# Two contraction stages cut into twice as many passes with operands loaded two passes ahead, and a shorter recurrence of powers

## The chip, the cores and the metric

The kernel runs on one Trainium2 chip, on all 8 of its cores at once. Each core has five engines: TensorE (PE: matmuls, with its weight loads PEld), VectorE (DVE), ScalarE (ACT), GpSimd (POOL) and SyncE (SP). The last two only issue DMAs here. The metric is the device time in microseconds of the slowest core, and lower is better. The cores don't exchange anything: each takes 2,048 of the 16,384 tokens.

## The reference

The input is x with 16,384 tokens of width 4,096 (H). Cut to what matters:

```python
xn = layernorm(x)
# attention-like part: S = 1024, F = 9984, G = 6
approx_up = xn @ up_w.T
delta = xn @ gate_w.T - local_point
keep = abs(delta) <= 2.5
out = approx_up @ local_approx_output.T
for m in 1..6:
    tmp = delta**m / m! * approx_up        # written with exp, log and the sign
    if m > 4: tmp = tmp * keep
    out = out + tmp @ fuse_weight[:, :, m - 1].T
s = out + (silu(xn @ ffn_gate_w.T) * (xn @ ffn_up_w.T)) @ ffn_down_w.T
# second part: base weights plus a mixture of low-rank experts
g = silu(xn @ W_base.T + b_base + moe(xn))
result = x + s * g
```

## The kernel before

The whole kernel is the function `build` of before.py. It has no scheduler: `Prog.emit` appends each instruction to the list of its engine in program order, with the semaphores that it waits for and those that it increments, and each engine works its list strictly in order. `dma` (line 154) is the helper behind every transfer, so all transfers have that line. SP's transfers go through a hardware queue. GpSimd's go through a software queue; it takes all loads that cast float32 weights to bfloat16, and the stores that add to what DRAM holds.

A core's data stand feature-major: 128 partitions of features or of contraction, 2,048 tokens along the free axis. `xnbuf` holds 32 blocks of 2,048 tokens in bfloat16. `wbufA` and `wbufB` hold weight tiles in turn, the PSUM tensors `P0` and `P1` (2,048 columns of float32 each) take the results of groups in turn. The stages, in order:

- ln and moe (from line 193): layer norm in place in `xnbuf`, the router and the low-rank part.
- g (line 444): g for 32 blocks of 128 output rows, to `g_d` in DRAM.
- B (line 510): for 8 blocks of S and 2 halves of the tokens (16 half-tiles) the matmuls of `approx_up` (L565) and `gate` (L580), then on VectorE the powers of delta times `approx_up`, each scaled and cast by ScalarE and stored by SP to `tmp_d`, seven operands of 8 blocks.
- D (line 675): for 78 blocks of F the gate and up matmuls (L722, L736), the product to `a_d`.
- C (line 778): the seven operands of `tmp_d` times `w7b`, contraction 7 x 1,024, into `s_d`.
- E (line 867): `a_d` times `wdb`, contraction 9,984, added into `s_d`, and in its last pass the result.

The whole of `tmp_d` or `a_d` doesn't fit into `xnbuf`, so C and E go in passes over the contraction. C has 2 passes (called C0 and C1 here) of 28 contraction blocks, E has 3 (E0 to E2) of 26. At the start of a pass SP loads its operands, filling nearly all of `xnbuf`, in 7 or 5 transfers; they wait for the last matmul of the pass before (`w_ops`). The pass then runs over 32 blocks of 128 output rows (`hc`). A group, which is one `hc` in one pass, has 4 x 28 matmuls (C, line 841) or 4 x 26 (E, line 942) into one PSUM tensor. Its weight tile is issued by `emit_cload` or `emit_eload` when group hc - 2 has ended; the tiles of the first two groups wait for the last group of the pass before:

```python
if hc >= 2:
    w.append(("MM", grp[hc - 2]))
else:
    w.append(("MM", t_mm_d_last if pz == 0 else gpp))
```

Behind each group ScalarE copies PSUM to the one staging tile `stf` (L856, L958), and GpSimd stores `stf` to `s_d[hc]`: plainly in C0, with `accum_op=ALU.add` in C1, E0 and E1. The copy waits for the store before it (`gs_tok[hc - 1]`), as there is one `stf`. On GpSimd's list the weight load for hc + 2 stands ahead of the store of hc.

In the last pass of E nothing is accumulated in DRAM. For each group SP loads `s_d`, `g_d` (into the last quarter of `xnbuf`) and `x_fm` (into `stf`), VectorE adds PSUM to s (L978), multiplies with g (L982), adds x (L985), and SP stores `stf` to `out`. The load of x into `stf` waits for the store of the group before (`os_out[hc - 1]`), the load of s for its last VectorE operation.

## Time and profile before

| what | value |
|---|---|
| three runs | 10157.4, 12016.82, 12089.78 us (median 12016.82) |
| profiled execution, time | 10159.01 us |
| its span on the slowest core | 10157.5 us |
| spans of the eight cores | 10128.5 to 10157.5 us |
| mean granted TensorE clock | 0.969 to 0.971 of full speed |
| busy in the span | PE 9528.4, PEld 4305.5, DVE 782.6, ACT 707.4, POOL 709.6 us |
| HBM | 917.81 MB read, 271.58 MB written per core |

The profiled execution stands with the fastest of the three runs. The span is from the first to the last instruction of a core; the launch adds little to it (1.5 us here). By the timeline D ends at about 6125 us, C0 starts at 6166, C1 at 7018, E0 at 7853, E1 at 8636, E2 at 9425.

How to read it: busy time of an engine matters only where that engine sets the pace. The list of waits says what ended an engine's idle time. In the timeline, pieces of equal instructions are merged, and "SPq" or "POOL ... DMA_DIRECT2D" is the issuing of a transfer, not the transfer itself; its landing is in the list of DMA issues, in us from the issue. KB there count what is written, so a cast weight tile reads twice that.

### The profile page before, as it was taken

To read this page: it belongs to the slowest core of one execution; us is meant where nothing else is said; L and a number is where in the kernel's file an instruction comes from. 1 tells how busy PE (TensorE), PEld (TensorE's weight loads), DVE (VectorE), ACT (ScalarE), POOL (GpSimd) and SP (SyncE) were. 2 spreads that over 40 slices of the span, in tenths; PEclk is the share of its full clock that TensorE was granted. 3 is DMA by queue.
4 is the path that set the end of the run, shared out by engine and by line. 5 is a ranking of instruction groups with operands and counts; after the bars stand their busy time and mean duration, and the time that the engine had idled before them with its cause. 6 is when DMAs were issued, how large, how long until landed. Compare 5 with 4: busy or idle time off the path is not lost.

```text
span 10157.5 us, 93330 instructions; the slowest of 8 cores (10128.5 to 10157.5 us)
## 1 busy us (share of the span) xinstructions
PE 9528.4 (94%) x43089; PEld 4305.5 (42%) x43960; DVE 782.6 (8%) x560; ACT 707.4 (7%) x510; POOL 709.6 (7%) x534
## 2 busy tenths in 40 slices
PE   4799989899999999999999997997997997998899
PEld 1344434344444444444444443443443443443344
DVE  1200035000000000000000000000000000000233
ACT  2000023000000000000000000000000000000000
POOL 0000000000000000000000000000100110010000
PEclk6899999999999999999999998998998998999999
DMA  5155565443443434434344435556566666566888
...
DMA packets 1486876, 822.07 MB, mean 81 GB/s; under 512 B 1403671, under 2 KB 1403928, under 8 KB 1449496
## 3 DMA queue, kind: packets, MB, share of 16 engines
...
q14 instruction: 41, 0.34, 0.0%
HBM read 917.81 MB, written 271.58 MB: 117 GB/s over the span
## 4 chain that ended last, share of the span: by engine, by line
PE 93%; another core or an unknown queue 2%; DMA 2%; DVE 1%; issue 1%; ACT 0%; SPq 0%; POOL 0%; DVEq 0%; ACTq 0%; POOLq 0%
PE P L942 21%; PE P L722 21%; PE P L736 21%; PE P L841 15%; PE P L478 9%; PE P L565 2%; PE P L580 2%; DMA xnbuf<-x_fm 1%; DVE xnbuf L292 0%; DVE xnbuf L298 0%; DMA xnbuf<-tmp_d 0%; ACT scr L213 0%; PE P L230 0%; DMA wbufA<-wub 0%
## 5 line engine op out<-in xcount | busy, mean ns | idle before, releaser
L942 PE MATMUL P<-xnbuf,wbufA 128*128 128x512 bf16 x4893 | 1086.9, 381 | 194.1 <-DMA wbufA<-wdb 188.9
L722 PE MATMUL P<-xnbuf,wbufA 128*128 128x512 bf16 x4893 | 1087.0, 380 | 37.4 <-DMA wbufA<-wub 32.2
L736 PE MATMUL P<-xnbuf,wbufA 128*128 128x512 bf16 x4892 | 1084.4, 379 | 5.3
L736 PE MATMUL P<-xnbuf,wbufB 128*128 128x512 bf16 x4892 | 1084.4, 379 | 5.3
L722 PE MATMUL P<-xnbuf,wbufB 128*128 128x512 bf16 x4892 | 1084.2, 379 | 5.3
L942 PE MATMUL P<-xnbuf,wbufB 128*128 128x512 bf16 x4892 | 1079.7, 379 | 5.3
L841 PE MATMUL P<-xnbuf,wbufA 128*128 128x512 bf16 x3513 | 781.2, 381 | 119.5 <-DMA wbufA<-w7b 103.2
L942 PEld LDWEIGHTS P<-xnbuf,wbufA 128*128 128x128 bf16 x4992 | 489.9, 98 | 783.9 <-issue 199.8
L841 PE MATMUL P<-xnbuf,wbufB 128*128 128x512 bf16 x3511 | 774.6, 379 | 3.8
L722 PEld LDWEIGHTS P<-xnbuf,wbufA 128*128 128x128 bf16 x4992 | 488.5, 98 | 623.8 <-issue 36.0
L736 PEld LDWEIGHTS P<-xnbuf,wbufA 128*128 128x128 bf16 x4992 | 488.9, 98 | 588.6
L736 PEld LDWEIGHTS P<-xnbuf,wbufB 128*128 128x128 bf16 x4992 | 488.9, 98 | 588.6
L942 PEld LDWEIGHTS P<-xnbuf,wbufB 128*128 128x128 bf16 x4992 | 488.5, 98 | 589.0
L722 PEld LDWEIGHTS P<-xnbuf,wbufB 128*128 128x128 bf16 x4992 | 488.0, 98 | 589.4
L841 PEld LDWEIGHTS P<-xnbuf,wbufA 128*128 128x128 bf16 x3584 | 351.6, 98 | 544.3 <-issue 125.8
L841 PEld LDWEIGHTS P<-xnbuf,wbufB 128*128 128x128 bf16 x3584 | 350.7, 98 | 422.9
L764 DVE TENSOR_TENSOR bfst<-scr,P 128x1024 bf16<-128x1024 f32 x156 | 190.5, 1221 | 4136.0 <-PE P L736 4136.0
L478 PE MATMUL P<-xnbuf,wbufA 128*128 128x512 bf16 x2007 | 452.0, 380 | 5.1 <-DVE scr L426 3.0
L478 PE MATMUL P<-xnbuf,wbufB 128*128 128x512 bf16 x2006 | 449.9, 379 | 2.2
L753 ACT ACTIVATE scr<-P 128x1024 f32<-128x1024 f32 x156 | 159.7, 1024 | 4151.4 <-PE P L722 4151.4
L978 DVE TENSOR_TENSOR xnbuf<-P,xnbuf 128x2048 f32<-128x2048 f32 x32 | 73.3, 2292 | 3800.0 <-PE P L942 3625.3
L478 PEld LDWEIGHTS P<-xnbuf,wbufA 128*128 128x128 bf16 x2048 | 200.9, 98 | 246.3 <-issue 6.3
...
## 6 DMA issues: line engine op xcount, KB each, us to landing
s_d<-stf POOLq DMA_DIRECT2D x128, 1024.0 KB, 13.1
wbufA<-wgb POOLq DMA_DIRECT2D x39, 1024.0 KB, 14.0
wbufA<-wub POOLq DMA_DIRECT2D x39, 1024.0 KB, 18.1
wbufB<-wgb POOLq DMA_DIRECT2D x39, 1024.0 KB, 14.0
wbufB<-wub POOLq DMA_DIRECT2D x39, 1024.0 KB, 18.0
...
```

What stands on the lines that cost most here:

```text
L478: lambda e, buf=buf, P=P, kc=kc, c0=c0: e.matmul(P[:, c0:c0 + 512], buf[:, kc * 128:(kc + 1) * 128], xn(kc, c0, 512), start=(kc == 0), sto ...
L565: e.matmul(P[:, pc:pc + 512], buf[:, kc * 128:(kc + 1) * 128], xn(kc, c0, 512), start=(kc == 0), stop=(kc == KC - 1)),
L580: e.matmul(P[:, pc:pc + 512], buf[:, 4096 + kc * 128: 4096 + (kc + 1) * 128], xn(kc, c0, 512), start=(kc == 0), stop=(kc == KC - 1)),
L722: pc=ntl * 512: e.matmul(P[:, pc:pc + 512], buf[:, kc * 128:(kc + 1) * 128], xn(kc, c0, 512), start=(kc == 0), stop=(kc == KC - 1)),
L736: pc=1024 + ntl * 512: e.matmul(P[:, pc:pc + 512], buf[:, 4096 + kc * 128: 4096 + (kc + 1) * 128], xn(kc, c0, 512), start=(kc == 0), stop= ...
L753: lambda e, P=P, sgs=sgs: e.activation(sgs, P[:, 0:1024], AF.Silu),
L764: e.tensor_tensor(abuf[:, t0:t0 + 1024], sgs, P[:, 1024:2048], ALU.mult),
L841: sp=(op == 6 and scl == 3): e.matmul(P[:, c0:c0 + 512], buf[:, j * 128:(j + 1) * 128], cop(j, c0, 512), start=st, stop=sp),
L942: e.matmul(P[:, c0:c0 + 512], buf[:, fsc * 128:(fsc + 1) * 128], cop(fsc, c0, 512), start=(fsc == 0), stop=(fsc == 25)),
L978: lambda e, P=P: e.tensor_tensor(s_ld, P[:, :], s_ld, ALU.add),
```

## The change

Four things are changed.

- C gets 4 passes of 14 contraction blocks, E 6 of 13. Group sizes are 4 x 14 and 4 x 13 matmuls, weight tiles 448 and 416 KB instead of 896 and 832. `w7b` and `wdb` are laid out on the host to fit.
- `xnbuf` is split into region A and region B. Pass n uses A if it is even, B if it is odd. The operands of the first two passes of a stage are issued at its start, and those of pass n + 2 behind pass n, waiting for its last matmul (`grp_pass[pz - 2]`). Semaphores LA and LB replace OL.
- The stores with accumulation are now those of C1 to C3 and E0 to E4; the final arithmetic is in E5. The weight tiles of a pass's first two groups wait, as before, for the last group of the pass before.
- In B each power comes from the product before it (`ts_b = delta * ts_a` and so on), without the separate chain of powers; the absolute value goes to `dpA`, right behind delta, and the mask is applied once to the fifth product.

```diff
-    w7b = nc.dram_tensor("w7b", [2, KC, 7, 4, 128, 128], F32, **EI)
+    w7b = nc.dram_tensor("w7b", [4, KC, 7, 2, 128, 128], F32, **EI)
...
-    wdb = nc.dram_tensor("wdb", [3, KC, 26, 128, 128], F32, **EI)
+    wdb = nc.dram_tensor("wdb", [6, KC, 13, 128, 128], F32, **EI)
...
+                t = p.emit("scalar", lambda e: e.activation(dpA, delta, AF.Abs),
+                           wait=[("AC", t_ac_delta)])
+                t_ac_abs = t["AC"]
                 tt = p.emit("vector", lambda e: e.tensor_mul(ts_a, delta, au_f),
                             wait=[("AC", t_ac_delta), ("EV", t_ev_auf)],
                             inc=[("EV", 1)])
                 t_ac1 = store_op(1, ts_a, tt["EV"])
-                p.emit("vector", lambda e: e.tensor_mul(dpA, delta, delta))
-                tt = p.emit("vector", lambda e: e.tensor_mul(ts_b, dpA, au_f),
+                tt = p.emit("vector", lambda e: e.tensor_mul(ts_b, delta, ts_a),
                             inc=[("EV", 1)])
                 t_ac2 = store_op(2, ts_b, tt["EV"])
-                p.emit("vector", lambda e: e.tensor_mul(dpB, dpA, delta))
-                tt = p.emit("vector", lambda e: e.tensor_mul(ts_a, dpB, au_f),
+                p.emit("vector",
+                       lambda e: e.tensor_single_scalar(dpA, dpA, 2.5,
+                                                        ALU.is_le),
+                       wait=[("AC", t_ac_abs)])
+                tt = p.emit("vector", lambda e: e.tensor_mul(ts_a, delta, ts_b),
                             wait=[("AC", t_ac1)], inc=[("EV", 1)])
                 t_ac3 = store_op(3, ts_a, tt["EV"])
-                p.emit("vector", lambda e: e.tensor_mul(dpA, dpB, delta))
-                tt = p.emit("vector", lambda e: e.tensor_mul(ts_b, dpA, au_f),
+                tt = p.emit("vector", lambda e: e.tensor_mul(ts_b, delta, ts_a),
                             wait=[("AC", t_ac2)], inc=[("EV", 1)])
                 t_ac4 = store_op(4, ts_b, tt["EV"])
-                p.emit("vector", lambda e: e.tensor_mul(dpB, dpA, delta))
-                t = p.emit("scalar", lambda e: e.activation(ts_b, delta, AF.Abs),
-                           wait=[("AC", t_ac4)])
-                t_ac_abs = t["AC"]
-                p.emit("vector",
-                       lambda e: e.tensor_single_scalar(ts_b, ts_b, 2.5,
-                                                        ALU.is_le),
-                       wait=[("AC", t_ac_abs)])
-                p.emit("vector", lambda e: e.tensor_mul(dpB, dpB, ts_b))
-                tt = p.emit("vector", lambda e: e.tensor_mul(ts_a, dpB, au_f),
+                p.emit("vector", lambda e: e.tensor_mul(dpB, delta, ts_b))
+                tt = p.emit("vector", lambda e: e.tensor_mul(ts_a, dpB, dpA),
                             wait=[("AC", t_ac3)], inc=[("EV", 1)])
                 t_ac5 = store_op(5, ts_a, tt["EV"])
-                p.emit("vector", lambda e: e.tensor_mul(dpA, dpB, delta))
-                tt = p.emit("vector", lambda e: e.tensor_mul(ts_b, dpA, au_f),
+                tt = p.emit("vector", lambda e: e.tensor_mul(ts_b, delta, ts_a),
                             wait=[("AC", t_ac4)], inc=[("EV", 1)])
                 t_ac6 = store_op(6, ts_b, tt["EV"])
...
+        def emit_c_oploads(pz):
+            reg = "AB"[pz % 2]
+            w = [("MM", grp_pass[pz - 2]), ("DBG", t_dbg_ln)]
+            w += [("TS%d" % i, t_ts_final[i]) for i in range(4)]
+            base = (pz % 2) * 28672
             for op in range(7):
-                sem_o = "OL%d" % op
+                sem_o = "L%s%d" % (reg, op)
                 tt = dma("sync", sem_o,
-                         xnbuf[:, op * 8192:(op + 1) * 8192].rearrange(
-                             "p (s t) -> p s t", s=4),
-                         tmp_d[op, pz * 4:(pz + 1) * 4].rearrange(
+                         xnbuf[:, base + op * 4096: base + (op + 1) * 4096]
+                         .rearrange("p (s t) -> p s t", s=2),
+                         tmp_d[op, pz * 2:(pz + 1) * 2].rearrange(
                              "s p t -> p s t"),
-                         wait=w_ops)
-                ol_tok[op] = tt[sem_o]
-
+                         wait=w)
+                ol_tok[(pz, op)] = (sem_o, tt[sem_o])
+
+        def emit_cwload(pz, hc, grp, wtok):
+            w = []
+            if hc >= 2:
+                w.append(("MM", grp[hc - 2]))
+            else:
+                w.append(("MM", grp_pass[pz - 1]))
+            buf = [wbufA, wbufB][hc % 2]
+            sem = ["WA", "WB"][hc % 2]
+            tt = dma("gpsimd", sem,
+                     buf[:, 0:1792].rearrange("p (j m) -> p j m", j=14),
+                     w7b[pz, hc].rearrange("o s p m -> p (o s) m"), wait=w)
+            wtok[hc] = tt[sem]
+
+        emit_c_oploads(0)
+        emit_c_oploads(1)
+        for pz in range(4):
+            base = (pz % 2) * 28672
...
+            emit_cwload(pz, 0, grp, wtok)
+            emit_cwload(pz, 1, grp, wtok)
...
+            if pz + 2 < 4:
+                emit_c_oploads(pz + 2)
...
+        grp_pass = {-2: c_regA_last, -1: c_regB_last}
...
+        def emit_e_oploads(tz):
+            reg = "AB"[tz % 2]
+            w = [("MM", grp_pass[tz - 2]), ("AS0", t_as_final[0]),
+                 ("AS1", t_as_final[1])]
...
+        for tz in range(6):
...
-                if tz < 2:
+                if tz < 5:
...
+            if tz + 2 < 6:
+                emit_e_oploads(tz + 2)
```

`emit_ewload` and the rest of `emit_e_oploads` are built like their twins in C.

Three places of the order of instructions, before and now. First SP, from the first operand load of C to the first load of the final arithmetic; `xnbuf<-tmp_d` are operands of C, `xnbuf<-a_d` of E. Before:

```order
L154 DMA xnbuf<-tmp_d 128x4x2048 [waits MM,TS0,TS1,TS2,TS3]
L154 DMA xnbuf<-tmp_d 128x4x2048 x6
L154 DMA xnbuf<-tmp_d 128x4x2048 [waits MM]
L154 DMA xnbuf<-tmp_d 128x4x2048 x6
L154 DMA xnbuf<-a_d 128x6x2048 [waits MM,AS0,AS1]
L154 DMA xnbuf<-a_d 128x5x2048 x4
L154 DMA xnbuf<-a_d 128x6x2048 [waits MM]
L154 DMA xnbuf<-a_d 128x5x2048 x4
L154 DMA xnbuf<-a_d 128x6x2048 [waits MM]
L154 DMA xnbuf<-a_d 128x5x2048 x4
L154 DMA xnbuf<-s_d 128x2048 [waits GS]
```

Now:

```order
L155 DMA xnbuf<-tmp_d 128x2x2048 [waits MM,TS0,TS1,TS2,TS3]
L155 DMA xnbuf<-tmp_d 128x2x2048 x13
L155 DMA xnbuf<-tmp_d 128x2x2048 [waits MM]
L155 DMA xnbuf<-tmp_d 128x2x2048 x6
L155 DMA xnbuf<-tmp_d 128x2x2048 [waits MM]
L155 DMA xnbuf<-tmp_d 128x2x2048 x6
L155 DMA xnbuf<-a_d 128x5x2048 [waits MM,AS0,AS1]
L155 DMA xnbuf<-a_d 128x4x2048 x2
L155 DMA xnbuf<-a_d 128x5x2048 [waits MM]
L155 DMA xnbuf<-a_d 128x4x2048 x2
```

Each load had waited for the end of the pass just before its own. Now the first wait covers two passes of C, and each later set stands behind the end of the pass two before its own. Four more pairs of rows with `xnbuf<-a_d`, for E2 to E5, follow in the second list.

Second GpSimd, from the last groups of C0 to the first groups of C1. Before:

```order
L154 DMA s_d<-stf 128x2048 [waits AC]
L154 DMA wbufB<-w7b 128x28x128 [waits MM]
L154 DMA s_d<-stf 128x2048 [waits AC] x3
L154 DMA wbufA<-w7b 128x28x128 [waits MM]
L154 DMA wbufB<-w7b 128x28x128
L154 DMA wbufA<-w7b 128x28x128 [waits MM]
L154 DMA s_d<-stf 128x2048 [waits AC]
```

Now:

```order
L155 DMA s_d<-stf 128x2048 [waits AC]
L155 DMA wbufB<-w7b 128x14x128 [waits MM]
L155 DMA s_d<-stf 128x2048 [waits AC] x3
L155 DMA wbufA<-w7b 128x14x128 [waits MM]
L155 DMA wbufB<-w7b 128x14x128
L155 DMA wbufA<-w7b 128x14x128 [waits MM]
L155 DMA s_d<-stf 128x2048 [waits AC]
```

Nothing has moved here: two weight tiles stand behind the last three stores. They have half the size, and the first still waits for TensorE's count. This piece now comes nine times in C and E instead of four.

Third VectorE, one half-tile of B, from the copy of `approx_up` (all names in it are parts of `scr`). Before:

```order
L631 TENSOR_TENSOR scr<-scr 128x1024 [waits AC,EV]
L635 TENSOR_TENSOR scr<-scr 128x1024 [waits EV]
L636 TENSOR_TENSOR scr<-scr 128x1024 [waits EV]
L639 TENSOR_TENSOR scr<-scr 128x1024 [waits EV]
L640 TENSOR_TENSOR scr<-scr 128x1024 [waits AC,EV]
L643 TENSOR_TENSOR scr<-scr 128x1024 [waits EV]
L644 TENSOR_TENSOR scr<-scr 128x1024 [waits AC,EV]
L647 TENSOR_TENSOR scr<-scr 128x1024 [waits EV]
L652 TENSOR_SCALAR scr<-scr 128x1024 [waits AC,EV]
L655 TENSOR_TENSOR scr<-scr 128x1024 [waits EV]
L656 TENSOR_TENSOR scr<-scr 128x1024 [waits EV]
L659 TENSOR_TENSOR scr<-scr 128x1024 [waits EV]
```

Now:

```order
L635 TENSOR_TENSOR scr<-scr 128x1024 [waits AC,EV]
L639 TENSOR_TENSOR scr<-scr 128x1024 [waits EV]
L643 TENSOR_SCALAR scr<-scr 128x1024 [waits AC,EV]
L646 TENSOR_TENSOR scr<-scr 128x1024 [waits AC,EV]
L649 TENSOR_TENSOR scr<-scr 128x1024 [waits AC,EV]
L652 TENSOR_TENSOR scr<-scr 128x1024 [waits EV]
L653 TENSOR_TENSOR scr<-scr 128x1024 [waits AC,EV]
L656 TENSOR_TENSOR scr<-scr 128x1024 [waits AC,EV]
```

Ahead of both stands the copy `scr<-P`, and behind the first one more multiplication, by `au_f` (L660). Five multiplications are gone; the comparison (TENSOR_SCALAR) moved from the ninth place to the third.

## Rows read from the trace of the kernel before

**Rows 1.** The page, its part 1: busy time and share of the span.
```profile
PE 9528.4 (94%) x43089; PEld 4305.5 (42%) x43960; DVE 782.6 (8%) x560; ACT 707.4 (7%) x510; POOL 709.6 (7%) x534
```

**Rows 2.** Waits of TensorE, whole span: total us, times, longest.
```profile
PE P L942 <- DMA wbufA<-wdb: 188.9, 3, 68.2
PE P L841 <- DMA wbufA<-w7b: 103.2, 2, 61.4
PE P L722 <- DMA wbufA<-wub: 32.2, 1, 32.2
PE P L841 <- DMA xnbuf<-tmp_d: 12.6, 3, 6.2
```

**Rows 3.** Timeline, C0 to C1: start us, us, engine, instruction, idle before.
```profile
6932.51 24.34 PE L841 MATMUL P<-xnbuf,wbufB 128*128 128x512 bf16 x110
...
6956.93 33.06 SPq L154 DMA_DIRECT2D xnbuf<-tmp_d  x7
...
6959.47 0.53 POOL L154 DMA_DIRECT2D s_d<-stf  x1 [23.59 <-ACT stf L856]
6960.24 1.56 POOL L154 DMA_DIRECT2D wbufA<-w7b  x1 [0.24 <-issue]
...
7018.24 26.50 PE L841 MATMUL P<-xnbuf,wbufA 128*128 128x512 bf16 x110 [61.39 <-DMA wbufA<-w7b]
```

**Rows 4.** Windows, that stall: busy us per engine, PEclk, DMA share, GB/s.
```profile
6957.00:7018.00 61.00, 0.00 (x0) 0.00 (x0) 0.00 (x0) 1.88 (x1) 3.65 (x3) 0.53 1.06 282
```

**Rows 5.** DMA issues of that stall, 6960 to 7030: KB each, us to landing.
```profile
wbufA<-w7b POOLq DMA_DIRECT2D x1, 896.0 KB, 57.7
```

**Rows 6.** Timeline, the end of B and the start of D.
```profile
1798.34 1.23 DVE L660 TENSOR_TENSOR scr<-scr 128x1024 f32<-128x1024 f32 x1
...
1812.16 16.52 PE L722 MATMUL P<-xnbuf,wbufA 128*128 128x512 bf16 x63 [32.21 <-DMA wbufA<-wub]
```

**Rows 7.** Timeline, one group end in C1.
```profile
7335.03 1.88 ACT L856 ACTIVATE stf<-P 128x2048 f32<-128x2048 f32 x1 [22.30 <-PE P L841]
7335.37 1.57 POOL L154 DMA_DIRECT2D wbufA<-w7b  x1 [20.92 <-PE P L841]
7337.47 0.87 POOL L154 DMA_DIRECT2D s_d<-stf  x1 [0.54 <-ACT stf L856]
```

**Rows 8.** DMA issues in C1, 7050 to 7770: KB each, median us to landing.
```profile
s_d<-stf POOLq DMA_DIRECT2D x29, 1024.0 KB, 14.7
...
wbufA<-w7b POOLq DMA_DIRECT2D x14, 896.0 KB, 11.7
```

**Rows 9.** DMA issues in E0, 7900 to 8480 us.
```profile
s_d<-stf POOLq DMA_DIRECT2D x26, 1024.0 KB, 13.8
```

**Rows 10.** DMA issues, 8554 to 8556: a store with no weight tile beside.
```profile
s_d<-stf POOLq DMA_DIRECT2D x1, 1024.0 KB, 7.8
```

**Rows 11.** Timeline, the last pass E2: one turn of the output loop.
```profile
9494.28 22.61 PE L942 MATMUL P<-xnbuf,wbufB 128*128 128x512 bf16 x102
...
9501.85 0.34 SPq L154 DMA_DIRECT2D out<-stf  x1
...
9510.23 0.33 SPq L154 DMA_DIRECT2D stf<-x_fm  x1
9516.73 22.61 PE L942 MATMUL P<-xnbuf,wbufA 128*128 128x512 bf16 x102
...
9517.67 2.29 DVE L978 TENSOR_TENSOR xnbuf<-P,xnbuf 128x2048 f32<-128x2048 f32 x1 [15.89 <-DMA stf<-x_fm]
...
9524.82 0.34 SPq L154 DMA_DIRECT2D out<-stf  x1
```

**Rows 12.** DMA issues in E2, 9430 to 10157 us.
```profile
out<-stf SPq DMA_DIRECT2D x32, 1024.0 KB, 7.2
...
stf<-x_fm SPq DMA_DIRECT2D x31, 1024.0 KB, 7.3
```

**Rows 13.** Waits of VectorE in E2: total us, times, longest.
```profile
DVE xnbuf L978 <- DMA stf<-x_fm: 174.6, 11, 17.0
```

155 lines of the change are left out of this document (74 added, 81 removed).

## The prediction

> **What bounds the kernel now.** I read the page first: TensorE is busy 94% of the span [rows 1], so only what stops TensorE, or what comes to stop it, can move the time. Next the waits of TensorE [rows 2]: stages C and E, which the change rewrites, lose 188.9 + 103.2 + 12.6 = 304.7 us to DMA. These are five stalls, one ahead of each of their five passes. The 32.2 us in the same list is the start of D and stays. Then the timeline around one stall [rows 3]. The last group of pass C0 ends at 6956.9 (6932.51 + 24.34). In that instant SP issues the operand loads of the next pass, and ScalarE evicts; then GpSimd issues the s_d store (6959.47) and behind it the weight loads (6960.24). TensorE restarts at 7018.24, 61.4 us late, released by its first weight tile. The DMA engines are full meanwhile, at 282 GB/s [rows 4]; most of it is SP's 14.7 MB of operands, and the 0.9 MB weight tile beside them needs 57.7 us to land [rows 5]. So the stall is one of bandwidth: its length follows the bytes that are released at the boundary.
>
> **B, the recurrence of powers.** VectorE does 14 operations per half-tile before and 9 after. The five that go are multiplications of 1.23 us; 16 half-tiles make 98 us of VectorE. TensorE waits for nothing but weights around B [rows 2], and the last VectorE operation of B starts at 1798.34, 13.8 us before D's first weights release TensorE at 1812.16 [rows 6]. The weight loads hide the edit: 0 us. Without that cover only the last half-tile's saving, 6 us, would show.
>
> **C and E, twice the passes.** C goes from 2 passes to 4, E from 3 to 6. A group (one block of 128 output rows in one pass) goes from 112 to 56 matmuls in C and from 104 to 52 in E, the matmuls in all stay the same, and so do bytes of weights and operands. Where TensorE paces, nothing is gained or lost: a C group takes 24.2 us now, 12.1 after; an E group 22.45 (9516.73 - 9494.28 [rows 11]), 11.2 after.
>
> **The boundaries.** There are 5 now and 10 after. The order of SP shows operands of pass n+2 released by the end of pass n, and that is the moment at which both first weight tiles of pass n+1 are released as well. These operands have a whole pass until they are needed, but they share the DMA engines with weights that are needed at once. In the C stall the bytes are 14.7 MB of operands + 1.05 of s_d + 0.92 of weights = 16.7 MB in 61.4 us, 0.27 MB/us. After: 7.3 + 1.05 + 0.46 = 8.8 MB, 32.7 us. The weight tile's own landing says the same: 57.7 / 2 + 3.3 us until its issue = 32.2 us. In E the bytes are 6.8 + 1.05 + 0.43 = 8.3 MB, 31 us. I take 32 us. Eight boundaries have that pattern (C0 to C1, and on until E3 to E4): 256 us. Ahead of C0 both operand halves (14.7 MB) are issued together; the third weight tile is held until the queue is dry, some 57 us after the start (15.6 MB at 0.27 MB/us), in which two groups run: 57 - 2 x 12.1 = 33 us. Ahead of E5 no operands are issued: the store leaves 2.6 us after the group's end and the small weight tile lands with it, by [rows 8, 10] some 12 us later: 15 us. Sum 33 + 256 + 15 = 304 us, against 304.7 now: 0. Bounds for each of the eight: 13 us (weights beside the store only, as ahead of E5) and 61 (nothing gained by the smaller loads), so -152 to +232 in all; the value is the one that two workings give.
>
> Each restart after such a stall runs at half the clock at first (granted 0.53 in the stall [rows 4], the level of 1.2 GHz): the first group took 26.50 us instead of 24.34 [rows 3], 2.2 us more. Five restarts more: +11 us (bounds 0 and 22).
>
> **The accumulation into s_d.** Every group stores once, so there are 288 stores instead of 128. There is one staging tile stf, so eviction, s_d store, next eviction is a loop of 1.88 us + 0.56 + landing [rows 7]. Behind a whole weight tile the store lands in 14.7 us in C [rows 8] and 13.8 in E [rows 9]; with none it needs 7.8 [rows 10]. The loop is thus 10.2 to 17.1 us, and it must fit into 12.1 and 11.2. GpSimd issues in order: weights(n+2), store(n), weights(n+3). The weight tile is issued 0.3 us after the group's end (7335.03) and lands 11.7 us later, the store 5.1 us behind it (7337.47 + 14.7 = 7352.2 against 7347.1) [rows 7, 8]. A halved tile should land in about 7.8 us, estimated between half and all of 11.7; the store then lands 0.3 + 7.8 + 5.1 = 13.2 us after the group's end, 1.1 us after the next group's end in C, 2.0 us in E. The next eviction starts that much late; its store is issued later too, but still lands 13.2 us after its group's end (8.8 us after its issue, 7.8 being the floor). So the lateness stays near 2 us and does not grow. TensorE writes two PSUM tiles in turn and would notice only 9 us of it (11.2 - 1.9). Value taken: 0, because both ends of the working leave the loop room. Bounds: 0, and (17.1 - 12.1) x 96 + (16.2 - 11.2) x 160 = 1280 us if the landing did not shorten at all.
>
> **The last pass of E.** This term decides. Each group there reads s_d, g_d and x and writes out, 4.2 MB, whatever its number of matmuls. stf takes x and then the result, so out store, x load and three VectorE operations are a loop: 9501.85 out issued, 9510.23 x issued, 9517.67 VectorE starts, 9524.82 out issued, 22.97 us [rows 11]. By the medians it is 7.2 + 7.3 (landings [rows 12]) + 7.15 (three operations of 2.29 with gaps) + 0.15 = 21.8 us. TensorE's 22.45 just covers that now; 11 turns already wait for x [rows 13]. After, TensorE needs 11.2 us and the loop paces: 31 x (21.8 - 22.45) = -20 us, and the first group is 11.2 us shorter: -31 us. But only a sixth of E's matmuls sits beside this loop instead of a third. The rest stands before it: five passes of 32 x 11.22 = 359 us instead of two of 718, +359 us. Together +328 us. Bounds: a turn of 20 us (half the weight traffic beside it) to 23, the turn of rows 11: +272 to +365.
>
> **Sum** against the profiled execution (span 10157.5, time 10159): B 0, boundaries 0, clock +11, s_d 0, last pass +328 = +339; span 10,497, time 10,500 us rounded, 1.034 of now. Of the three runs shown one took 10,157.4, as the profiled one, and two over 12,000, which makes the median 12,016.8; the forecast is for an execution like the profiled one.
>
> **The rivals.**
> 1. The prefetch does what double buffering should. The operand loads leave room for the weight tile, and the eight boundaries shrink to 13 us: 33 + 104 + 15 = 152 us instead of 304, so 10,500 - 152 = 10,348 us: not slower by over 2%. It decides from the point where the first weight tile lands within 14 us of the last group's end. For it: nothing waits for the operands any more. Against: rows 3 and 5; one event releases both loads, and the large one wins. Two pages of the Trainium skill stand on the two sides. "Trainium Kernel Development and Optimization", Best Practices, advises double buffering to overlap DMA with compute; taken at its word it gives this rival's 10,348. "DMA: Bandwidth & Descriptors", section "Queues, rings and completion order", says that a DMA engine alternates between its queues packet by packet; with SP's large packets beside small ones the weights then stay slow for as long as SP's queue holds work, which gives the forecast's 10,500. The trace so far agrees with the second, with its 57.7 us.
> 2. The stf loop paces the eight accumulating passes. If the landing stays near 10.5 us, the loop is 12.9 us: 96 x 0.8 + 160 x 1.7 = 349 us more, 10,850 us. For it: DMA must finish twice as many stores in the same time. Against: it corrects itself, as above.
> 3. The last pass shrinks much further: a turn of 17 us, 150 us less, 10,350 us. Against: 7.2, 7.3 and 7.15 us are serial.
>
> **How the numbers follow.** Forecast 0.60, rival 1 0.12, rival 2 0.20, rival 3 0.03, none of these 0.05. A measurement of this kernel tells about 2% from no change, so slower begins at 10,362. Rivals 1 and 3 hold 0.15, most of it above 9,956 us; faster than that would need all stalls gone and the last pass halved: 0.02, within 2%: 0.14, slower: 0.84. The range for 8 in 10 reaches down to rival 1 and up to rival 2: 10,345 to 10,860 (the forecast's own: 10,430 to 10,620).
>
> **What would show it.** Right: ten waits of TensorE for weights in C and E, eight of them 28 to 37 us, their sum near 300; groups 12.1 and 11.2 us apart in C and E0 to E4, with ScalarE waiting 1 to 2 us for the s_d store; in E5 VectorE waiting for x in nearly every turn, turns 21 to 22 us apart, and TensorE waiting over 300 us for VectorE; B and D of unchanged length. Wrong: an E5 much shorter than 690 us (last term), boundaries below 20 us (rival 1), TensorE waiting for ScalarE inside passes (rival 2), or a B that ends earlier.

## The result, and the profile after

The changed kernel is slower: 1.0352 times the time of the kernel before (95% interval 1.0307 to 1.0396). Its least disturbed executions took 10,506 to 10,519 us against 10,157.4 and 10,157.5 before. The medians over all ten executions of each kernel are 11,427 and 11,715 us, since in many of them one or both dies ran at a lower clock; the ratio and the numbers below are from cores that did not. Of the changed kernel the views are of core 4 (span 10,508.8 us, clock 0.957), beside core 4 of before (10,133.8 us). Over all such cores the median span is 10,499 us, before 10,142 us.

The page of core 4, from its parts 1 and 3 (busy time; bytes):

```profile
PE 9659.0 (92%) x43960; PEld 4319.4 (41%) x43960; DVE 684.6 (7%) x480; ACT 1007.8 (10%) x670; POOL 971.2 (9%) x854
...
HBM read 917.81 MB, written 439.35 MB: 129 GB/s over the span
```

Beside [rows 1]: VectorE has lost 98 us and 80 instructions (B), ScalarE has gained 160 copies, GpSimd 320 instructions: 160 stores and 160 weight tiles. HBM writes rose by 168 MB, which is 160 stores of 1.05 MB; reads are what they were.

Then the waits of TensorE on core 4, which answer to [rows 2]:

```profile
PE P L959 <- DVE stf L1003: 216.9, 29, 9.2
PE P L959 <- DMA wbufA<-wdb: 210.0, 6, 39.5
PE P L842 <- DMA wbufA<-w7b: 109.4, 4, 37.3
...
PE P L718 <- DMA wbufA<-wub: 30.7, 1, 30.7
PE P L842 <- DMA xnbuf<-tmp_d: 30.7, 7, 12.3
```

The first line is new: in the last pass TensorE now waits for VectorE. The second and third hold the stalls for weights ahead of nine of the ten passes, and 0.7 us for the third tile of C0; the last line is the start of C0, which waits for its operands in seven pieces. With 0.3 us for the second tile of E5 they make 350.4 us; core 4 of before has 292.8 (core 6, on which the forecast was made, 304.7).

The timeline around the end of C0, beside [rows 3]:

```profile
6534.51 7.55 SPq L155 DMA_DIRECT2D xnbuf<-tmp_d  x7
6534.63 1.88 ACT L859 ACTIVATE stf<-P 128x2048 f32<-128x2048 f32 x1 [10.21 <-PE P L842]
6537.04 0.53 POOL L155 DMA_DIRECT2D s_d<-stf  x1 [11.50 <-ACT stf L859]
6538.00 1.10 POOL L155 DMA_DIRECT2D wbufA<-w7b  x1 [0.42 <-issue]
...
6569.65 14.56 PE L842 MATMUL P<-xnbuf,wbufA 128*128 128x512 bf16 x56 [35.22 <-DMA wbufA<-w7b]
```

The order is that of before: in the instant in which the pass ends SP issues seven operand loads, the weights follow 3.5 us later, and TensorE restarts 35.2 us late on a weight tile. The stall fell from 61.4 to 35.2 us (57.6 on core 4 of before), but this happens eight times now. Three more of the eight, and the stall ahead of E5:

```profile
6996.16 14.64 PE L842 MATMUL P<-xnbuf,wbufA 128*128 128x512 bf16 x56 [37.26 <-DMA wbufA<-w7b]
...
7421.71 15.19 PE L842 MATMUL P<-xnbuf,wbufA 128*128 128x512 bf16 x56 [36.23 <-DMA wbufA<-w7b]
...
7848.38 14.33 PE L959 MATMUL P<-xnbuf,wbufA 128*128 128x512 bf16 x52 [36.78 <-DMA wbufA<-wdb]
...
9830.55 13.12 PE L959 MATMUL P<-xnbuf,wbufA 128*128 128x512 bf16 x52 [19.03 <-DMA wbufA<-wdb]
```

(The other four, ahead of E1 to E4, are 38.82, 38.87, 39.49 and 37.02 us.)

The last pass, beside [rows 11], one turn of the output loop on core 4:

```profile
10106.49 0.34 SPq L155 DMA_DIRECT2D out<-stf  x1
...
10111.31 0.33 SPq L155 DMA_DIRECT2D stf<-x_fm  x1
10120.04 2.29 DVE L996 TENSOR_TENSOR xnbuf<-P,xnbuf 128x2048 f32<-128x2048 f32 x1 [13.62 <-PE P L959]
...
10127.19 0.34 SPq L155 DMA_DIRECT2D out<-stf  x1
10127.27 13.24 PE L959 MATMUL P<-xnbuf,wbufB 128*128 128x512 bf16 x52 [7.35 <-DVE stf L1003]
```

The result is stored, x loaded 4.8 us later into the same `stf`, VectorE works, the next result is stored: 20.7 us in this turn, 21.0 as the mean of the pass. The view puts VectorE's wait of 13.62 us down to TensorE; but the group that VectorE reads here is the one before, which had ended at 10098.6, so the wait was for x, as in 30 of the 32 turns by the list of waits. TensorE stands beside this loop: it waits 7.35 us for VectorE to give PSUM back. E5 takes 678 us from its first matmul to the end; E2 of before, with twice the matmuls, took 733.

Two pieces of windows show what lies between (busy us per engine, granted clock, DMA share, GB/s):

```profile
8700.00:9000.00 300.00, 300.00 (x1392) 135.98 (x1391) 0.00 (x0) 49.34 (x27) 54.23 (x53) 1.00 0.99 132
9860.00:10460.00 600.00, 387.05 (x1487) 157.91 (x1485) 195.71 (x86) 0.00 (x0) 31.54 (x28) 0.83 0.76 219
```

Inside an accumulating pass TensorE is busy in all 300 of 300 us, though the DMA engines are busy 0.99 of the time (0.61 in the same stretch of the kernel before); in the last pass it is busy 387 of 600.

**Where the time came from**, core 4 against core 4, from the starts of the first matmuls of the passes and the stalls ahead of these:

| piece | before | after | difference |
|---|---|---|---|
| stage C without stalls | 1556 | 1561 | +5 |
| stalls in and ahead of C | 110.5 | 140.1 | +30 |
| stalls ahead of passes of E | 182.3 | 210.3 | +28 |
| passes of E ahead of the last, without stalls | 1441 | 1809 | +368 |
| last pass of E | 733 | 678 | -55 |

They sum to +376 us; the spans differ by 375.0. So B, D and all that stands ahead of C give nothing, and the extra time is that of E, in which the matmuls taken out of the last pass have to be done outside it while the last pass hardly shrinks.

### The profile page after: what moved, and what is told of

Same layout as the page of the kernel before. It is cut to its first block, busy times and chain, and to the rows that moved or that the text cites. A ratio compares the mean times of both kernels' runs of the same rounds, so it can differ in the third digit from the quotient of the medians.

```text
span 11235.5 us, 94837 instructions; the slowest of 8 cores (10474.6 to 11235.5 us)
## 1 busy us (share of the span) xinstructions
PE 10332.0 (92%) x43089; PEld 4490.9 (40%) x43960; DVE 684.8 (6%) x480; ACT 1007.5 (9%) x670; POOL 970.2 (9%) x854
## 4 chain that ended last, share of the span: by engine, by line
PE 72%; DMA 20%; ACT 3%; DVE 3%; issue 2%; POOL 0%; SPq 0%; ACTq 0%; DVEq 0%; POOLq 0%
PE P L718 21%; PE P L732 21%; PE P L842 14%; DMA s_d<-stf 12%; PE P L479 10%; ACT stf L976 3%; PE P L566 2%; PE P L581 2%; DMA stf<-x_fm 2%; DMA wbufA<-wdb 1%; DMA out<-stf 1%; DMA xnbuf<-x_fm 1%; DMA wbufA<-w7b 1%; PE P L959 1%; DVE xnbuf L1000 1%
## 5 line engine op out<-in xcount | busy, mean ns | idle before, releaser
L959 PE MATMUL P<-xnbuf,wbufA 128*128 128x512 bf16 x4893 | 1127.8, 389 | 314.3 <-DMA wbufA<-wdb 205.8
L959 PE MATMUL P<-xnbuf,wbufB 128*128 128x512 bf16 x4892 | 1121.8, 387 | 115.8 <-DVE stf L1003 110.2
L718 PE MATMUL P<-xnbuf,wbufA 128*128 128x512 bf16 x4893 | 1192.6, 406 | 37.4 <-DMA wbufA<-wub 30.6
L732 PE MATMUL P<-xnbuf,wbufA 128*128 128x512 bf16 x4892 | 1190.8, 405 | 6.9
L718 PE MATMUL P<-xnbuf,wbufB 128*128 128x512 bf16 x4892 | 1190.6, 405 | 6.9
L732 PE MATMUL P<-xnbuf,wbufB 128*128 128x512 bf16 x4892 | 1190.0, 405 | 7.0
L842 PE MATMUL P<-xnbuf,wbufA 128*128 128x512 bf16 x3511 | 791.7, 383 | 144.2 <-DMA wbufA<-w7b 106.7
L959 PEld LDWEIGHTS P<-xnbuf,wbufA 128*128 128x128 bf16 x4992 | 496.7, 100 | 933.3 <-issue 372.5
L718 PEld LDWEIGHTS P<-xnbuf,wbufA 128*128 128x128 bf16 x4992 | 514.1, 103 | 703.5 <-issue 386.4
L959 PEld LDWEIGHTS P<-xnbuf,wbufB 128*128 128x128 bf16 x4992 | 495.9, 100 | 729.0 <-issue 163.6
L842 PE MATMUL P<-xnbuf,wbufB 128*128 128x512 bf16 x3513 | 779.9, 379 | 3.7
L718 PEld LDWEIGHTS P<-xnbuf,wbufB 128*128 128x128 bf16 x4992 | 513.8, 103 | 671.4 <-issue 354.3
L732 PEld LDWEIGHTS P<-xnbuf,wbufA 128*128 128x128 bf16 x4992 | 513.5, 103 | 671.6 <-issue 354.3
L732 PEld LDWEIGHTS P<-xnbuf,wbufB 128*128 128x128 bf16 x4992 | 513.3, 103 | 671.1 <-issue 352.2
L842 PEld LDWEIGHTS P<-xnbuf,wbufA 128*128 128x128 bf16 x3584 | 352.2, 98 | 574.3 <-issue 158.9
L479 PE MATMUL P<-xnbuf,wbufA 128*128 128x512 bf16 x2007 | 546.6, 438 | 6.5 <-DVE scr L427 3.0
L479 PE MATMUL P<-xnbuf,wbufB 128*128 128x512 bf16 x2006 | 544.8, 436 | 3.7
L842 PEld LDWEIGHTS P<-xnbuf,wbufB 128*128 128x128 bf16 x3584 | 350.7, 98 | 422.9
L976 ACT ACTIVATE stf<-P 128x2048 f32<-128x2048 f32 x160 | 300.3, 1877 | 1695.7 <-DMA s_d<-stf 1474.5
L859 ACT ACTIVATE stf<-P 128x2048 f32<-128x2048 f32 x128 | 240.3, 1877 | 1474.5 <-DMA s_d<-stf 871.2
## 6 DMA issues: line engine op xcount, KB each, us to landing
wbufA<-wgb POOLq DMA_DIRECT2D x39, 1024.0 KB, 13.8
```

The costliest lines, as they stand in the source:

```text
L479: lambda e, buf=buf, P=P, kc=kc, c0=c0: e.matmul(P[:, c0:c0 + 512], buf[:, kc * 128:(kc + 1) * 128], xn(kc, c0, 512), start=(kc == 0), sto ...
L718: pc=ntl * 512: e.matmul(P[:, pc:pc + 512], buf[:, kc * 128:(kc + 1) * 128], xn(kc, c0, 512), start=(kc == 0), stop=(kc == KC - 1)),
L732: pc=1024 + ntl * 512: e.matmul(P[:, pc:pc + 512], buf[:, 4096 + kc * 128: 4096 + (kc + 1) * 128], xn(kc, c0, 512), start=(kc == 0), stop= ...
L842: sp=(op == 6 and scl == 1): e.matmul(P[:, c0:c0 + 512], buf[:, j * 128:(j + 1) * 128], xnbuf[:, base + j * 2048 + c0: base + j * 2048 + c ...
L859: lambda e, P=P: e.activation(stf[:, :], P[:, :], AF.Copy),
L959: e.matmul(P[:, c0:c0 + 512], buf[:, fsc * 128:(fsc + 1) * 128], xnbuf[:, base + fsc * 2048 + c0: base + fsc * 2048 + c0 + 512], start=(fs ...
```

## The experiments

Twelve kernels were run. All figures are spans of cores chosen as above, lowest to highest, with their median; the kernel before, run beside them on the same three chips, has 10,113 to 10,160 (median 10,142), the changed kernel 10,464 to 10,547 (median 10,499).

| kernel | spans of cores, us | median |
|---|---|---|
| b_alone | 10,202 to 10,287 (see there) | 10,243 |
| c_alone | 10,137 to 10,209 | 10,153 |
| hold | 10,497 to 10,565 | 10,521 |
| spread | 10,359 to 10,431 | 10,384 |
| spread_roll | 10,266 to 10,326 | 10,294 |
| stf2 | 10,439 to 10,492 | 10,474 |
| no_sg | 10,352 to 10,425 | 10,398 |
| twoset | 10,355 to 10,498 | 10,468 |
| all3 | 10,199 to 10,332 | 10,261 |
| deep8 | 10,316 to 10,388 | 10,349 |
| deep_spread | 10,314 to 10,394 | 10,332 |
| deep_spread_twoset | 10,156 to 10,199 | 10,174 |

### Which part of the change costs: B alone, C alone

**b_alone**: the kernel before with the new recurrence. One of its lines:

```diff
-                p.emit("vector", lambda e: e.tensor_mul(dpA, delta, delta))
-                tt = p.emit("vector", lambda e: e.tensor_mul(ts_b, dpA, au_f),
+                tt = p.emit("vector", lambda e: e.tensor_mul(ts_b, delta, ts_a),
```

> The kernel before with only the new recurrence of stage B. Theory (B is covered by TensorE and by D's first weights): 10,157 us as before, within 10 us. Rival (VectorE's shorter chain lets D start earlier or takes its 98 us off the path): 10,060 us, or D's first matmul over 10 us earlier.

Its cores had granted clocks of 0.956 to 0.963, where the kernel before mostly has 0.969 to 0.971, so it is compared at equal clock: at 0.962 to 0.963 four of its cores took 10,202 to 10,216 us, and two of the kernel before on the same chip 10,205 and 10,215. The window of B, on core 7 of b_alone:

```profile
1330.00:1800.00 470.00, 442.44 (x2012) 198.57 (x2011) 167.93 (x144) 161.99 (x144) 25.72 (x16) 0.96 0.53 96
```

VectorE works 167.9 us in it; the kernel before has 265.9 us there on core 4, with 441.9 of TensorE. 98 us of VectorE went and TensorE's share stayed: the edit is worth nothing, since nobody waited for VectorE there.

**c_alone**: C in four passes with two operand regions as changed, E as before.

> The kernel before with only stage C in 4 passes and two regions; E keeps its 3 passes, each with all its operands loaded at its start. Theory (cost sits in E's last pass, boundaries about cancel): C boundaries 31, 35, 37 and 36 us as in the changed kernel, E boundaries near 59, 62 and 68 as before, sum 328 against 305, two more slow restarts 4 us: 10,157 + 27 = 10,184 us. Rival (the cost comes from more passes and more s_d stores in any stage, so C pays its share): 2 of the 5 extra passes of the changed kernel's +351 us, 140 us: 10,300 us.

It took what the kernel before takes, within about 11 us at the median. My figure for it was some 30 us too high, and the timeline of core 3 shows at which boundary most of that lies:

```profile
6598.48 16.03 PE L848 MATMUL P<-xnbuf,wbufA 128*128 128x512 bf16 x56 [32.82 <-DMA wbufA<-w7b]
...
7107.53 15.79 PE L848 MATMUL P<-xnbuf,wbufA 128*128 128x512 bf16 x56 [37.21 <-DMA wbufA<-w7b]
...
7592.95 16.96 PE L848 MATMUL P<-xnbuf,wbufA 128*128 128x512 bf16 x56 [13.82 <-DMA wbufA<-w7b]
```

(The granted clock of this core was 0.899, so its groups take longer; its first two stalls for DMA, 32.82 and 37.21 us, are like those of the changed kernel.) Ahead of C3 no operands are released in this kernel, because E still loads its own at the end of C, and the stall is 13.82 us where the changed kernel has 36.23. That is a small experiment of its own: same weights, same store, with the operands or without them 36 or 14 us. With B and C at nothing, the loss lies in E. E alone was not run; this is by subtraction and by the table above, which agree.

### The boundaries: what is released, and when

**hold**: each operand set is issued when group 2 of the pass before its own has ended, all of it at once, instead of at the boundary.

```diff
                 if hc + 2 < KC:
                     emit_ewload(tz, hc + 2, grp, wtok)
+                if hc == 2 and tz < 5:
+                    emit_e_oploads(tz + 1, grp[2])
...
-            if tz + 2 < 6:
-                emit_e_oploads(tz + 2)
```

> The changed kernel with each set of operand loads released not by the end of a pass but by the end of group 2 of the next pass, all transfers of the set at once. Theory (the boundary stall is the weight tile queued beside the operands): the stall at eight boundaries falls from 37.5 us to 16 to 20 us, as ahead of E5 (19 us). Its second half: the bytes still hold up a weight tile, now the one of group 4 or 5, so a new stall of about 20 us appears inside each pass, and the time stays near 10,500 us. Rival (only the boundary is critical, inside a pass the two groups of lead hide the loads): no new stall, 8 x 19 us less, 10,350 us.

No gain. The timeline of core 3 shows where the stall went:

```profile
6563.84 14.01 PE L861 MATMUL P<-xnbuf,wbufA 128*128 128x512 bf16 x56 [11.36 <-DMA wbufA<-w7b]
...
6631.50 14.31 PE L861 MATMUL P<-xnbuf,wbufA 128*128 128x512 bf16 x56 [17.39 <-DMA wbufA<-w7b]
```

The boundary fell from 35 to 11 us here (to 14 or 15 us ahead of C2, C3 and E0, and to 16 to 20 us ahead of E1 to E5), and a few groups later, where the 7 MB are issued now, TensorE waits 17 us for weights. The first group behind either stall takes 14.0 or 14.3 us instead of 12.25. So a boundary wait is not bound to the boundary: it goes with the burst of operands.

**spread**: the same set in seven transfers, one behind each of groups 2, 6, ..., 26 (for E the 13 blocks are cut into seven pieces for it).

```diff
+                if hc % 4 == 2 and hc < 30 and tz < 5:
+                    emit_e_oploads(tz + 1, grp[hc], [hc // 4])
```

> The changed kernel with the operand transfers of the next pass released one by one, after groups 2, 6, 10 and so on to 26 (E's in 7 transfers instead of 3). Theory (the bytes cost nothing if they come in small pieces between weight tiles): boundaries 16 to 20 us, no stall inside passes, about 8 x 19 + 5 = 157 us less than the changed kernel: 10,350 us. Rival (the DMA engines have no room inside a pass: share 0.84 in C and 0.92 in E in the changed kernel): each piece of 1 MB holds up groups by 2 to 4 us, and the time stays above 10,450 us.

Now 10,384, 115 us less than the changed kernel, on the side of the theory (10,350) but 34 us above it. Its waits (core 0):

```profile
PE P L962 <- DVE stf L1008: 194.2, 29, 8.2
PE P L962 <- DMA wbufA<-wdb: 151.1, 31, 24.0
...
PE P L861 <- DMA wbufA<-w7b: 38.5, 3, 13.7
```

In C the waits for weights went from 109.4 us to 38.5. In E they became 31 instead of 6, 151.1 us instead of 210.0: six at the boundaries (13.3 us ahead of E0, 18.5 to 24.0 us ahead of the others) and 25 small ones of 0.2 to 4.6 us in the passes, where the DMA engines are at a share of 0.91 to 0.92.

**spread_roll**: as spread, and the first two weight tiles of a pass are issued behind groups 30 and 31 of the pass before, as soon as their buffer is free, and not at the end of the pass.

```diff
                 if hc + 2 < KC:
                     emit_ewload(tz, hc + 2, grp, wtok)
+                elif tz < 5:
+                    emit_ewload(tz + 1, hc + 2 - KC, grp, nxt, grp[hc])
```

> The spread kernel (operand transfers one by one inside a pass) and besides the first two weight tiles of each pass issued after groups 30 and 31 of the pass before, in the rhythm of all others. Theory (what was left of each boundary, 11 to 14 us in C and about 20 in E, was the weight tile issued only after the last group): boundaries near 0 in C, under 8 us in E; eight of 16 us, 19 ahead of E5 and nine restarts of 2.3 us, 165 us less than the spread kernel: 10,215 us on an undisturbed core. Rival (E's passes are short of DMA, share 0.94, so what is taken from the boundary comes back as waits inside E's passes): no gain in E, about 50 us less: 10,330 us.

10,294, another 90 us less, between the two figures. The boundaries are nearly gone (2.3 to 6.1 us, once 8.8), now released by ScalarE, and what stays stands inside the passes (core 4, E0):

```profile
7724.78 13.07 PE L967 MATMUL P<-xnbuf,wbufA 128*128 128x512 bf16 x52 [3.83 <-ACT stf L902]
...
7864.30 13.07 PE L967 MATMUL P<-xnbuf,wbufA 128*128 128x512 bf16 x52 [2.66 <-DMA wbufA<-wdb]
...
8101.02 12.97 PE L967 MATMUL P<-xnbuf,wbufA 128*128 128x512 bf16 x52 [5.23 <-ACT stf L988]
```

E0 lasts 371 us where TensorE needs 359. The waits shown cost more than they last, since the group behind each takes some 13 instead of 11.39 us; behind others, one of 2.84 us among them, the group takes 11.38.

### The staging tile

**stf2**: the copies and stores to `s_d` use two staging tiles in turn, with a semaphore each.

```diff
+                    sg, gsem = [(stf[:, :], "GS"), (scr[:, 0:2048], "GZ")][hc % 2]
+                    w = [("MM", grp[hc]), (gsem, p.val(gsem))]
```

> The changed kernel with two staging tiles (and two semaphores) for the s_d stores of C and E0 to E4. Theory (ScalarE's 2,335 us of waiting for the s_d store are hidden behind TensorE's second PSUM tile): the waits shrink, the time stays at 10,500 us within 15. Rival (the loop of eviction and store sets part of the pace or delays the boundaries): 30 us or more less.

10,474 against 10,499: 25 us less, more than the theory's 15 and less than the rival's 30. ScalarE's waits for the store (1444.4 us in the changed kernel's E, 890.1 in C) are gone from the list, it waits for TensorE instead. Inside the passes their lateness was hidden by the two PSUM tensors, as forecast. At the ends of E's passes it was not. The end of E1 on core 4, first in the changed kernel, then in stf2:

```profile
8610.93 1.85 SPq L155 DMA_DIRECT2D xnbuf<-a_d  x3
8614.36 1.88 ACT L976 ACTIVATE stf<-P 128x2048 f32<-128x2048 f32 x1 [8.63 <-DMA s_d<-stf]
...
8617.51 1.49 POOL L155 DMA_DIRECT2D wbufA<-wdb  x1
```

```profile
8621.60 1.48 SPq L155 DMA_DIRECT2D xnbuf<-a_d  x3
8621.74 1.88 ACT L976 ACTIVATE scr<-P 128x2048 f32<-128x2048 f32 x1 [9.35 <-PE P L959]
...
8624.67 1.49 POOL L155 DMA_DIRECT2D wbufA<-wdb  x1
```

In the changed kernel the copy of the last group waits for the store before it and starts 3.5 us after the group's end (8610.86). The first weight tile of the next pass stands behind the store of that copy in GpSimd's list, so it is issued 6.7 us after the end; with two staging tiles it is 3.1 us. Ahead of E1 to E5 the issue comes 5.6 to 6.9 us after the end in the changed kernel and 3.1 to 3.4 us in stf2, and the five stalls sum to 173.2 and 158.5 us. These 15 us are most of the 16.4 us by which the span of core 4 shrank. So a long list of waits of an engine that is not the bound (2,334 us here) may be worth next to nothing, but not quite nothing where something urgent stands behind it.

### The last pass

**no_sg**: the last pass loads s and g for its first group only and uses these for all 32; the computation of the output leaves out the loads of 31 of 32 blocks of `s_d` and `g_d`. This takes 2.1 of the 4.2 MB of a group away, and keeps the chain store, load of x, three VectorE operations.

```diff
+                    if hc == 0:
+                        dma("sync", "EL", s_ld, s_d[hc, :, :], wait=wl)
+                        dma("sync", "EL", g_ld, g_d[hc, :, :],
+                            wait=[("GT", t_gt_final)])
```

> The changed kernel whose last pass loads s and g only for the first group and reuses them (the output of the other groups is left out in that respect), so that the out store and the x load have the DMA engines nearly alone. Theory (the turn of 21.1 us is made of transfers that share bandwidth plus 7.15 us of VectorE): out store 4 us, x load 5 to 6, turn 17 us, 31 x 4 = 125 us less than the changed kernel. Rival (fixed latency of the serial steps): turn stays above 20 us.

10,398, 101 us less at the median, a third of the 319 us (678 - 359) by which the last pass exceeds TensorE's work. One turn on core 7:

```profile
10102.14 0.34 SPq L155 DMA_DIRECT2D out<-stf  x1
...
10107.97 0.33 SPq L155 DMA_DIRECT2D stf<-x_fm  x1
10113.19 2.29 DVE L998 TENSOR_TENSOR xnbuf<-P,xnbuf 128x2048 f32<-128x2048 f32 x1 [11.15 <-DMA stf<-x_fm]
...
10120.34 0.34 SPq L155 DMA_DIRECT2D out<-stf  x1
```

18.2 us here and 17.5 in the next; the median landing of x is 5.3 us after its issue and not 8.5. The turn thus depends on both: half of its bytes gone took some 3 us off it, and 17.5 to 18.2 us are the serial chain with the transfers almost alone (5.8 + 5.2 + 7.15).

**twoset**: the changed kernel with two whole sets of s, g and x tiles in turn, the result written into the x tile, and the loads of the group after next issued as soon as its set is free. This takes the chain away and leaves the bytes.

```diff
+        sets = [(xf32[:, SLD:SLD + 2048], xf32[:, GLD:GLD + 2048],
+                 xf32[:, GLD + 2048:GLD + 4096]),
+                (scr[:, 0:2048], scr[:, 2048:4096], scr[:, 4096:6144])]
...
-                    dma("sync", "EL", s_ld, s_d[hc, :, :], wait=wl)
+                    if hc + 2 < KC:
+                        emit_finals(hc + 2)
```

> The changed kernel with only the last pass rearranged: two sets of tiles for s, g and x (the second in scr, which is free there), the result stored from the x tile, loads of group n+2 released by group n. Theory (the one staging tile makes out store, x load and VectorE serial, 21.1 us a turn): the turn falls to what the DMA engines need for 4.2 + 0.43 MB, 16 us at 0.285 MB/us, so 31 x 5 = 158 us less than the changed kernel, 10,350 us on an undisturbed core. Rival (the pass was bound by DMA bandwidth already): the turn stays above 20 us, 10,480 us or more.

The theory's 10,350 was wrong for all but one core (core 3 of the profiled run, 10,355): the median is 10,468, 31 us less. But the reason is not simply that the bytes bind. Waits of TensorE for the weights of E, whole span, and then DMA issues of the last pass, both of core 4:

```profile
PE P L974 <- DMA wbufA<-wdb: 309.1, 12, 39.6
PE P L974 <- DMA wbufB<-wdb: 132.2, 7, 31.3
```

```profile
out<-scr SPq DMA_DIRECT2D x14, 1024.0 KB, 8.5
scr<-s_d SPq DMA_DIRECT2D x14, 1024.0 KB, 13.3
scr<-g_d SPq DMA_DIRECT2D x14, 1024.0 KB, 15.4
...
wbufB<-wdb POOLq DMA_DIRECT2D x14, 416.0 KB, 30.4
```

The wait for VectorE (216.9 us) is gone, and 231 us of waits for weights have come (309.1 + 132.2 less the 210.3 of before the edit). With six loads of SP outstanding, a weight tile of 0.43 MB needs 30.4 us to land instead of 6.4. It looks like the mechanism of the boundaries again, now inside the pass. From 9880 to 10440 us the DMA engines move 220 GB/s at a share of 0.83, so they are not full: while TensorE waits for its weight tile, VectorE and the loads behind it wait for TensorE.

**all3**: spread_roll and twoset together.

> Operands spread, weights in rhythm, and two sets of tiles in the last pass. Theory (the gains add up: 10,215 - 158 us): 10,060 us on an undisturbed core, below the kernel before (10,140 to 10,158). Rival (E short of DMA): 10,170 us, no better than before.

10,261, only 34 us less than spread_roll, and above what either side expected. Its waits on core 4 are twoset's: 162.9 us for `wbufA`, 137.4 for `wbufB`. What was still open was whether the last pass can be made short at all.

### More weights ahead

**deep8**: the changed kernel with eight weight slots (four in each of `wbufA` and `wbufB`), each loaded eight groups ahead, across the ends of passes.

```diff
+        def slot(q):
+            return [wbufA, wbufB][(q // 4) % 2], (q % 4) * 2048
...
+                emit_wload(pz * 32 + hc + 8, grp[hc])
```

> The changed kernel with eight weight slots in wbufA and wbufB instead of two, tile n+8 issued when group n has ended, also across passes; operand loads stay released by the end of a pass. Theory (the boundary stall is only the weight tile that queues beside the operands): seven tiles are in hand at a boundary, 8 stalls of 37 us, the 19 us ahead of E5 and their slow restarts go, 10,505 - 340 = 10,165 us on an undisturbed core. Rival (the s_d stores on the same queue starve too and hold ScalarE and then TensorE): 10 to 20 us stay at each boundary, 10,260 to 10,340 us.

10,349 at the median, 150 us less than the changed kernel, but not the theory's 10,165, and rather at or above the upper end of the rival's. No wait for weights is left at the boundaries; instead (core 4):

```profile
8701.55 1.88 ACT L965 ACTIVATE stf<-P 128x2048 f32<-128x2048 f32 x1 [15.46 <-DMA s_d<-stf]
8703.68 46.75 PE L949 MATMUL P<-xnbuf,wbufA 128*128 128x512 bf16 x208 [16.93 <-ACT stf L965]
```

TensorE runs into the next pass, and then ScalarE can't copy, as the store of `stf`, the other client of GpSimd's queue, is stuck behind the operands: with a full PSUM pair TensorE waits 16.9 us for it. (The granted clock of this core was 0.914.) The burst takes whatever is urgent beside it, and removing the first victim shows the next. It is not only the boundaries:

```profile
PE P L949 <- ACT stf L965: 124.0, 82, 17.8
```

Five of these 82 waits, of 11.7 to 17.8 us, stand near the starts of passes and make 80 us; nearly all the others are under 2 us and inside the passes of E, where in the changed kernel TensorE never waited for ScalarE. C adds 49.4 us in 7 waits.

**deep_spread**: deep8 with the operands spread as in spread.

> Eight weight slots and operand transfers one by one inside a pass. Theory (what spread_roll still lost, boundaries of 2 to 4 us and 17 us inside each E pass, was late weight tiles): 10,285 - 9 x 3 - 5 x 15 = 10,180 us on an undisturbed core, the floor for the last pass as it is. Rival (E's accumulating passes are at the limit of the DMA engines): no gain over spread_roll, 10,280 us.

10,332, only 17 us below deep8 and 37 us above spread_roll, also above the figures of both. Eight spans are all that there is of it, and its profile has none of these cores, so I draw no more from it than that spreading and depth do not add up. What stands in the way in its sibling is below.

**deep_spread_twoset**: and the two sets of tiles in the last pass.

> The same with two sets of tiles in the last pass. Theory (in twoset the freed loads crowded out the weight tiles, of which TensorE had only one in hand; with seven in hand the turn can fall to the bytes, 16 us): 31 x 4 us less than deep_spread, 10,060 us on an undisturbed core, under the kernel before. Rival (small weight packets get too little of the engines on the average, not only at times): the turn stays near 20 us, 10,160 us or more.

10,174: the rival's side, yet the fastest of all versions with twice the passes in C and E. Waits of TensorE and the window of the last pass on core 4:

```profile
PE P L967 <- ACT stf L985: 104.7, 44, 11.9
...
PE P L967 <- DMA wbufA<-wdb: 35.7, 3, 21.2
```

```profile
9680.00:10170.00 490.00, 376.32 (x1599) 161.63 (x1597) 217.74 (x95) 0.00 (x0) 25.91 (x23) 0.89 1.03 289
```

This settles twoset. With weights eight groups ahead the two sets save 157 us (deep_spread to deep_spread_twoset); with two tiles they save 31 to 34. The last pass takes 516 us instead of 678 and runs at 289 GB/s, with the DMA engines full (share 1.03). The bytes then set its length: 32 groups of 4.2 MB and weights of 0.43 MB are 148 MB, 513 us at this rate. TensorE's 359 us of E5 do not reach it. In the same window a weight tile lands 98 to 115 us after its issue; up to eight of them are outstanding on GpSimd's queue, so this time holds the wait behind the others. TensorE's waits for them are 58 us in the whole of E (35.7 and, for `wbufB`, 22.5), for they are issued eight groups ahead. The first line is the wait that is left in the accumulating passes: TensorE waits 104.7 us for ScalarE, whose one staging tile is still being stored. Eight weight slots with two staging tiles were not run.

No version beats the kernel before. The best stands 32 us (0.3%) above it, which is no difference by this measurement. The same cures could be applied to the kernel before without the twofold passes; that was not tried.

## Why the prediction came near, and which of its terms failed

The forecast was a span of 10,497 us for an execution like the profiled one, 1.034 of before; the cores of the changed kernel have 10,464 to 10,547, and the ratio is 1.035. The median over all executions, 11,427 us, lies above the range given (10,345 to 10,860), whose sum has no term for any execution unlike the profiled one. Within the sum the step that failed is the length of the boundaries. By its steps:

- **B, 0 us.** Right: b_alone at equal clock is the kernel before, and VectorE's 98 us are gone. The last VectorE operation of B now starts 20.4 us ahead of the first matmul of D (1778.82 to 1799.22), where it was 13.8 us on core 6 [rows 6] and 9.7 on core 4; D waits for its weights 30.7 us, before 28.1 (core 4) and 32.2 us (core 6).
- **The eight boundaries, 32 us each.** The mechanism is right (hold, spread and c_alone's C3 show it from three sides), the size too small: 35.2 to 39.5 us, 299.7 in all against 256, and five of the eight are above the 28 to 37 us given. Both parts of the working fell short. The landing, 57.7 / 2 = 28.9 us there, measured 30.9 to 33.7: in five of the stalls the DMA engines moved 233 to 258 GB/s, where they had 282 [rows 4], and the store in the burst lands in 9.7 to 13.5 us, no sooner than before (9.7 to 13.1). Why the shorter burst has the lower rate no run isolates. The 3.3 us until the weights' issue measured 3.1 to 3.6 up to E0 but 5.7 to 6.9 us ahead of E1 to E4; that is the lateness of the `stf` loop, as stf2 shows. Ahead of E5, 19.3 us for 15, it is the same: 5.6 us until the issue. In all, the term came to 350 us where 304 was forecast, +46, or +58 against the same core of before.
- **Ahead of C0, 33 us.** It measured 31.4 us, but by luck: the forecast let TensorE wait for the third weight tile, and it waited 0.7 us for that and 30.7 us, in seven pieces, for its first operands.
- **Restart at low clock, 2.2 us each.** About right: the first groups take 13.0 to 15.2 us against 11.4 in E and 12.25 in C, so 1.6 to 2.9 us. The clock granted from 6569 to 6584 was 0.82, in the stall ahead of it 0.54.
- **The loop through `stf`, 0 us.** Right inside the passes: from 8700 to 8800 us the copy starts 2.4 to 3.3 us after the group's end (2.0 forecast), and TensorE never waits for it. Wrong at their ends, where no second PSUM tensor hides it: there it costs about 15 us in all (stf2, core 4), and they sit in the boundaries above.
- **The last pass, -31, and the five passes ahead of it, +359.** The turn was forecast as 21.8 us and measured 21.0, so the pass shrank by 55 and not 31 us: 24 us in the changed kernel's favour. The five passes gained 368, of which some 9 are restarts. This is the term that decides, and its reasoning held: half of the matmuls left the pass, and its end came only 55 us nearer. One sign was missed: TensorE waits 216.9 us for VectorE and not over 300, since its groups mostly take 13 to 14 us there instead of 11.2 (granted clock 0.83 from 9860 to 10460).
- **The sum.** +58 from the boundaries and -24 from the last pass cancel in part: core 4 gained 375 us, the median 357, and 339 was forecast. So the total was better than its parts.

The rivals. **1**, that loads two passes ahead leave room for the weights: refused by stalls of 35 to 39 us, and by the runs. Its 13 us were seen only where no operands are released (c_alone) or where they are issued later (hold, spread). The Trainium skill, page "Trainium Kernel Development and Optimization", section "Best Practices", advises double buffering to overlap DMA with compute. The operands were double-buffered here and the stalls stayed; 14 us of stall instead of 36 came with a change of the release, not of the buffers. The weight tile of 0.43 MB needs 6.4 us in the last pass of the changed kernel and 30.4 us with six of SP's megabytes outstanding (twoset). In the stall of rows 3 (6950 to 7018 us, core 6) SP's 14.68 MB are 3,696 packets by the profile's count and GpSimd's 2.53 MB are 5,955, some 4.0 and 0.42 KB each. The Trainium skill, page "DMA: Bandwidth & Descriptors", section "Queues, rings and completion order", says that an engine alternates between its queues packet by packet. The slow landing beside SP's large packets fits this; that the queues alternate so is not itself shown. **2**, the `stf` loop paces: did not happen inside the passes of the changed kernel, but the same loop came up as the next wait once weights no longer stopped TensorE first: 124.0 us in the E of deep8 (16.9 us of it at one boundary) and 104.7 in that of deep_spread_twoset. **3**, a last pass with a turn of 17 us: 21.0, and 17.5 to 18.2 only with half of the bytes taken away.

The theories of the experiments were mostly too optimistic: by 34 us in spread, by 79 in spread_roll, by 114 to 201 in twoset, all3, deep8, deep_spread and deep_spread_twoset. In the last five it was in the same way: I priced the wait that the edit removes and not the one that stood behind it, mostly on the same DMA engines.

Open is why one core of twoset (core 3 of the profiled execution, 10,355) gained nearly five times as much as the median: its last pass ran at 259 GB/s, and TensorE waited 368 us for E's weights and not 441, but what let it is not shown. Open is also why deep_spread is hardly faster than deep8. The wait for ScalarE that deep_spread_twoset has in E is the likely reason, and two staging tiles would test it.
